# One half row tile of a graph attention kernel loaded as 120 rows and 8 rows

## What is computed

```python
h = input @ W
a1 = a[:D_OUT, 0]
a2 = a[D_OUT:, 0]
e = (h @ a1)[:, None] + (h @ a2)[None, :]
e = jnp.where(e > 0, e, ALPHA * e)
e = jnp.where(adj > 0, e, NEG)
attention = jax.nn.softmax(e, axis=1)
h_prime = attention @ h
return jax.nn.elu(h_prime)
...
x = _layernorm(x + _L0_gnn_ref(x, adj, L0_gnn_W, L0_gnn_a), axis=-1)
```

## Time and profile before

| what | us |
|---|---|
| three runs: median (lowest to highest) | 719.73 (718.51 to 720.04) |
| the profiled execution | 722.26 |
| its span, first to last instruction | 720.5 |
| PE busy in the span | 558.7 (78%) |
| ACT busy | 520.8 (72%) |
| DVE busy | 482.4 (67%) |
| POOL busy | 440.6 (61%) |
| loads and stores, HBM | 399 GB/s over the span |

### The profile page before, as it was taken

The page is one execution under the profiler, slowest core; times in us unless marked ns, Lnnn a source line. Parts: engine busy times, 40 slices in busy tenths (PEclk is TensorE's granted clock), DMA queues, the critical chain, the costliest instruction groups (busy, mean ns, idle before and its releaser), DMA issues.

```text
span 720.5 us, 11885 instructions
## 1 busy us (share of the span) xinstructions
PE 558.7 (78%) x3023; PEld 356.0 (49%) x3071; DVE 482.4 (67%) x2059; ACT 520.8 (72%) x414; POOL 440.6 (61%) x668
## 2 busy tenths in 40 slices
PE   0867887777777888787777988877777888787794
PEld 0333455444455555555445655554455555554483
DVE  1376677785766667777776567777766667776754
ACT  0847777777887878787887778787877878777410
POOL 2015457766766676767666576667766676776731
PEclk9978999997999988999998788999999988998955
DMA  8999999999999999999999999999999999999062
GB/s 351 328 417 429 425 421 428 428 423 425 427 428 426 427 428 426 425 429 425 427 429 426 428 425 428 426 429 428 425 425 430 428 426 428 425 426 407 24 171 80
DMA packets 34582, 285.57 MB, mean 396 GB/s; under 512 B 5512, under 2 KB 13856, under 8 KB 18048
## 3 DMA queue, kind: packets, MB, share of 16 engines
q1 hardware_dynamic: 29008, 276.83, 91.9%
q0 software_dynamic: 5120, 8.42, 3.3%
q10 hardware_dynamic: 432, 0.07, 0.1%
HBM read 283.18 MB, written 4.19 MB: 399 GB/s over the span
## 4 chain that ended last, share of the span: by engine, by line
DMA 71%; ACT 11%; PE 10%; issue 5%; DVE 2%; SPq 1%; ACTq 0%; POOLq 0%; POOL 0%; DVEq 0%
DMA adj_sb<-in_adj 68%; ACT adj_squared L558 10%; PE fold L660 5%; DMA a_sb<-in_L_gnn_a 2%; PE x_att_ps L713 1%; PE misc L685 1%; PE small L694 1%; PE fold L656 1%; SPq L402 1%; PE fold L757 1%; PE small L675 1%; PE x_att_ps L716 0%; DVE spread L376 0%; DVE stats L1000 0%; DVE x_sb L996 0%
## 5 line engine op out<-in xcount | busy, mean ns | idle before, releaser
L558 ACT ACTIVATE adj_squared<-adj_sb 128x4096 bf16<-128x4096 int32 x128 | 462.6, 3614 | 114.3 <-DMA adj_sb<-in_adj 111.7
L660 PE MATMUL fold<-adj_sb,bit_ident 128*128 128x512 bf16 x993 | 301.7, 448 | 9.1 <-DMA adj_sb<-in_adj 3.8
L503 POOL DMA_INDIRECT nb<-in_x,index x160 | 165.1, 1032 | 94.7 <-issue 68.7
L660 PEld LDWEIGHTS fold<-adj_sb,bit_ident 128*128 128x128 bf16 x1024 | 110.0, 107 | 151.6 <-issue 63.1
L868 DVE MAX8 top_map<-fold 128x8 f32<-128x512 f32 x128 | 89.5, 699 | 69.2 <-PE fold L660 64.3
L656 PE MATMUL fold<-col_no,ident_bf 128*128 128x512 bf16 x112 | 46.7, 417 | 111.3 <-DMA adj_sb<-in_adj 104.0
L364 POOL TENSOR_SCALAR edge_row<-row_iota,edge_in 128x128 f32<-128x128 int32 x186 | 128.1, 702 | 0.0
L382 POOL TENSOR_TENSOR spread<-edge_row,edge_w 128x384 f32<-128x384 f32 x60 | 54.4, 925 | 80.6 <-DVE edge_w L984 80.5
L656 PEld LDWEIGHTS fold<-col_no,ident_bf 128*128 128x128 bf16 x128 | 16.3, 127 | 131.8 <-issue 90.1
L483 POOL TENSOR_SCALAR empty_diag<-ident,counts 128x128 f32<-128x128 f32 x64 | 39.1, 616 | 59.6 <-DVE counts L904 32.7
L713 PEld LDWEIGHTS x_att_ps<-spread,nb 128*128 128x128 f32 x372 | 59.1, 226 | 9.2 <-issue 4.2
(11 more groups left out here) (120 smaller groups left out, 629.3 us busy)
## 6 DMA issues: line engine op xcount, KB each, us to landing
adj_sb<-in_adj SPq DMA_DIRECT2D x127, 2048.0 KB, 14.7
out<-x_sb SPq DMA_DIRECT2D x2, 1536.0 KB, 10.3
nb<-in_x,index POOLq DMA_INDIRECT x160, 2.4
adj_sb<-in_adj SPq DMA_DIRECT2D x2, 1024.0 KB, 16.1
out<-x_sb SPq DMA_DIRECT2D x5, 128.0 KB, 3.4
out<-x_sb SPq DMA_DIRECT2D x1, 384.0 KB, 10.0
W_sb<-in_L_gnn_W ACTq DMA_DIRECT2D x1, 64.0 KB, 7.8
x_sb<-in_x SPq DMA_DIRECT2D x4, 0.5 KB, 17.6
```

Of the source, the lines that this page charges most:

```text
L503: nc.gpsimd.indirect_dma_start(out=nb_of(j, g)[:, c, :], out_offset=None, in_=x[:, :], in_offset=bass.IndirectOffsetOnAxis(ap=index[:, g, ...
L558: nc.scalar.activation(adj_squared[:, h % 2, :], adj_sb[:, h % LOAD_SLOTS, :], ACT.Square, accum_out=half_sum[:, h:h + 1]).then_inc(square ...
L660: last = nc.tensor.matmul(fold[:, h % LOAD_SLOTS, :], bit_ident[:, b, :], adj_low[:, h % LOAD_SLOTS, b * FOLD:(b + 1) * FOLD, 0], start=Fa ...
```

## The change

The half (15, 0) is loaded by two DMAs instead of one: rows 0 to 119 and rows 120 to 127. The 120 rows raise the slot's own semaphore, and the 8 rows raise a new one, `rows_loaded`. ACT and PE wait for both before they square and fold that half. The load of 120 rows uses 15 DMA engines and that of 8 rows uses 8.

```diff
+        rows_loaded = sem("rows_loaded")
...
+        FEWER = P - P // 16
+        is_cut_half = lambda i, h: isinstance(i, int) and (i, h) == (BODIES - 1, 0)
...
+                        if is_cut_half(i, h):
+                            for lo, hi in ((0, FEWER), (FEWER, P)):
+                                nc.sync.dma_start(adj_sb[lo:hi, h % LOAD_SLOTS, :], adj_tiles[i * BODY, lo:hi, 0:HALF]
+                                                  ).then_inc(rows_loaded if lo else loaded[h % LOAD_SLOTS], 16)
+                            continue
                         parts = 2 if is_final(i, g) and h == HALVES - 1 else 1
...
                     act.wait_ge(loaded[h % LOAD_SLOTS], landings(i, h))
+                    if is_cut_half(i, h):
+                        act.wait_ge(rows_loaded, 16)
...
                     pe.wait_ge(loaded[h % LOAD_SLOTS], landings(i, h))
+                    if is_cut_half(i, h):
+                        pe.wait_ge(rows_loaded, 16)
```

## The result

The changed kernel takes 730.31 us (median of 6 runs, 728.84 to 732.16), the one before 719.04 us beside it (6 runs). The ratio is 1.0159, with a 95% interval from 1.0139 to 1.0179: slower by 11.3 us. The forecast was 717.2 us, faster by 2.5. The profiled execution took 730.26 us, its span is 728.5. The profiled execution before, 722.26 us, lies 3.2 us above the median of its kernel, and that of the changed kernel lies on it, so the two spans differ by only 8.0 us.

The account below looks back on a forecast made before the run. The DMA stream was taken as the bound, one engine about 3 us late. Relieving it, -3.1 + 0.6 = -2.5 us, with other terms at 0, took the median 719.73 to 717.2 us; range 715.8 to 722.3.

Parts of the forecast that it names:

- the path: From the late engine's part of half 5, landing at 660.98 us, some 60 us of work follow to the end.
- the price that no row showed: Load of 120 rows in half (15, 0): engines sharing write places; bounds 0 and 4.9 us, taken as 0.
- The bound of 4.9 us: Upper price of the 120-row load: eight rows per engine at half pace if two engines share a write place.
- rival A: Load of 120 rows: pairs of engines share write places; in full 2.4 us slower, 722.1 us; chance 0.25, in part 0.10.
- The wide case: Load of 120 rows: four engines meet instead of two, price 15 us; a small chance, outside the range.
- Part 1: Half (15, 0): one engine gets no rows of the 120; if the late one, it goes from 3 us late to 1.9 early.
- Rival B: Load of 120 rows: the late engine still gets its eight rows, nothing is gained, 719.7 to 720.3 us; chance 0.15.
- The hint that the lateness comes from the instruction queues: Queues q8 and q14 moved 0.26 MB in 22 packets, 9.7 us of one engine, more than enough for 3 us.
- Part 2: Load of 8 rows in half (15, 0): one row more on each of eight engines, later landings at worst 0.61 us behind.
- Parts 3 and 4: One more DMA issue on SP, 0.4 us but covered; two more waits on ACT and PE, 0 to 0.04 us, taken as 0.
- The gain that was forecast: Half 5 lands 2.5 us earlier, and all 2.5 us go through to the end of the kernel.

Follow-up runs that it names:

- cut_body2: The changed kernel with its cut moved to half (2, 0), some 525 us earlier, and nothing near the end: 729.01 us, ratio 1.0125 to the kernel before.
- near8: The kernel before plus, ahead of half (15, 0), one load of 8 rows into a spare buffer at partitions 120 to 127: 722.88 us, ratio 1.0047.
- only120: The changed kernel without the load of rows 120 to 127 of half (15, 0) or the wait for it: 728.54 us, ratio 1.0144 to the kernel before.
- only64_mid: The kernel before with only rows 32 to 95 of half (15, 0) loaded, 1 MB, the other 64 left out: 717.61 us, ratio 0.9977.
- extra7: The kernel before plus, ahead of half (15, 0), four loads of 7 rows into a spare buffer, partitions four apart: 722.17 us, ratio 1.0035.

## Why the prediction was wrong

**The bound and the path were read rightly.** The stream of loads bounds the kernel, one engine is about 3 us late, and the end hangs on half 5. In the changed kernel the chain leaves DMA at the same half, and cut_body2 shows that a loss in the stream goes through to the end.

**The step that failed is the price that no row showed**, "I take 0, the nearest row being the neighbouring 2 MB loads at full pace". Those rows are of loads of 128 partitions, and what the change alters is just that shape. It was a row near by in size and far away in kind. The bound of 4.9 us above it was too low as well. "Each row of the pair takes twice as long" was right: 213 GB/s over 16 engines are 13.3 each, 1.23 us for a row in place of 0.61, and the slow rows of the trace took about that. But I let only the eight rows of the half itself go at half pace. The hole lasted 15 us and not 9.8, because the neighbouring halves are drawn in: 196 slow rows where the half has 128. At half 5 the fifteenth increment came 7.6 us later (665.32 for 657.73) and that of the late engine 10.1, a further 2.5 us for which no run has a reason. So rival A was the right mechanism at 0.25, with 2.4 us for an outcome of 11.3. The wide case, a price of 15 us, which I left outside the range, was nearer, but by luck: it supposed rows at a quarter of the pace, and they went at half for longer.

**Part 1 failed too.** "If the one that is left out is the late one" was false: the lone stretch stayed and grew. Rival B was true at the same time as A. I had treated them as alternatives, and they were independent. By the sum each alone would have removed the gain. The hint that the lateness comes from the instruction queues holds, for q14.

**Part 2** (0.61 us for one row more) was mis-sized. The eight rows at partitions 120 to 127 cost 3.4 us (2.0 to 4.8) by near8; the 1.8 us by only120 are not clear of noise. By the map of the Trainium skill (SBUF — State Buffer, Door 1: The DMA port swizzle) four engines meet there at each of two places. Parts 3 and 4, the second issue and the two waits, cost nothing that shows: SP issued the two loads of half (15, 0) at about 618 us, 0.4 us apart, and no engine had landed its share before 634.

**The gain that was forecast** would have been smaller in any case. only64_mid takes 2.45 us out of the stream and lands the last part at 668.35, 2.4 us earlier; its time falls by 1.7 us (ratio 0.9977, so 0.1 to 3.1 us). I had let 2.5 us go through whole. The lower end of my range, 715.8 us, doesn't follow from its own terms either: 719.7 less 3.2 and less 1 is 715.5.

## What to carry to other kernels

Load in shapes of 128 partitions when the DMA stream is the bound. A cut by columns cost nothing that twelve runs could tell; a load of rows 0 to 111, 0 to 119 or 0 to 63 halves the pace for longer than the load itself, and neither a lone small load at the last eight partitions nor an early place in the kernel makes it cheap. When an engine is late, find out which it is by small extra loads before giving another engine less work. Read GB/s beside the busy share, which stays at 1.0 while the pace is half.

## What was not expected of the hardware

- 64 partitions can have the full pace: rows 32 to 95 went at 426 GB/s, rows 0 to 63 at 200.
- 128 KB in eight rows at partitions 120 to 127 cost 3.4 us (2.0 to 4.8) and made a hole, while 448 KB in 28 rows, seven engines each at its own place (extra7), cost 2.5 us (1.2 to 3.9) and made none. The 2.5 us are four rows' time of one engine.
- Rows of the loads next to an ill-placed one slow down with it: 118 slow rows around a load of 64.
- The late engine was one of the low-numbered, 2 or 3 (by the numbering of the Trainium skill). An instruction packet of 8 KB, 0.33 us long, made the row behind it take 1.27 us, and the 0.98 us so lost were never made up.
